# Attention scores of a two-block Macaron network: 32-row matmuls in the exponential pass and a mask matmul in the max pass

## What is computed

```python
def attn(x, wq, wk, wv, wo, bo):            # T = 2048, 16 heads, 8 numbers a head
    q, k, v = split_heads(x @ wq), split_heads(x @ wk), split_heads(x @ wv)
    scores = jnp.einsum('bhqd,bhkd->bhqk', q, k)
    scores = jnp.where(tril(ones((T, T))), scores, -jnp.inf)
    attn = softmax(scores / sqrt(8), axis=-1)
    return merge(jnp.einsum('bhqk,bhkd->bhqd', attn, v)) @ wo + bo
# the second attention is the same, with biased projections and without wo
```

## Time and profile before

| | |
|---|---|
| Time, median of 3 runs | 1313.72 us (1313.71 to 1315.61) |
| Span of the profiled execution | 1311.0 us, first to last instruction |
| Median of the runs above that span | 2.7 us |
| TensorE busy | 1194.1 us, 91% |
| VectorE busy | 1044.4 us, 80% |
| ScalarE busy | 723.5 us, 55% |
| Mean granted TensorE clock | 0.975 of full speed |

### The profile page before, as it was taken

The page is one execution under the profiler, slowest core; times in us unless marked ns, Lnnn a source line. Parts: engine busy times, 40 slices in busy tenths (PEclk is TensorE's granted clock), DMA queues, the critical chain, the costliest instruction groups (busy, mean ns, idle before and its releaser), DMA issues.

```text
span 1311.0 us, 21446 instructions
## 1 busy us (share of the span) xinstructions
PE 1194.1 (91%) x7781; PEld 510.1 (39%) x7781; DVE 1044.4 (80%) x3015; ACT 723.5 (55%) x861; POOL 66.6 (5%) x64
## 2 busy tenths in 40 slices
PE   1999958999999999999699979599999999999997
PEld 1455533333333333334455537233333333333336
DVE  8976588999999887875447567799999989878764
ACT  1322115566777777777332224156667777777773
POOL 5111010000000000000101000100000000000000
PEclk9999979999999999999799989799999999999999
DMA  4100142000000000000000000510000000000001
GB/s 147 34 1 1 39 131 58 2 1 2 2 1 1 2 1 2 1 1 2 1 0 1 1 1 25 154 48 2 2 1 2 2 1 1 2 1 2 2 2 33
DMA packets 23510, 23.26 MB, mean 18 GB/s; under 512 B 3134, under 2 KB 21220, under 8 KB 23404
## 3 DMA queue, kind: packets, MB, share of 16 engines
q1 hardware_dynamic: 22252, 18.73, 4.9%
q0 software_dynamic: 1152, 3.15, 0.9%
HBM read 13.20 MB, written 8.39 MB: 16 GB/s over the span
## 4 chain that ended last, share of the span: by engine, by line
PE 70%; DVE 22%; issue 4%; ACT 2%; DMA 1%; SPq 0%; DVEq 0%; ACTq 0%
PE psum L1184 18%; PE psum L1204 17%; PE psum L1164 14%; PE psum L442 9%; DVE part_max L1314 8%; PE psum L466 2%; PE psum L903 2%; PE psum L1171 2%; DVE junk L1320 2%; DVE xn L167 1%; DVE norm_v L150 1%; PE psum L1224 1%; PE psum L918 1%; DVE norm_stats L141 1%; PE psum L427 1%
## 5 line engine op out<-in xcount | busy, mean ns | idle before, releaser
L1275 ACT ACTIVATE hidden<-psum,exp_scale 128x1024 f32<-128x1024 f32 (+3 forms) x640 | 597.7, 984 | 258.9 <-PE psum L1164 137.3
L1314 DVE TENSOR_REDUCE part_max<-psum 128x1 f32<-128x512 f32 x768 | 492.1, 686 | 59.1 <-PE psum L1204 53.9
L1204 PE MATMUL psum<-k_slots,q_slots 128*128 128x512 f16 (+3 forms) x1280 | 401.2, 356 | 34.2 <-DVE part_max L1314 12.2
L1164 PE MATMUL psum<-q_slots,k_slots 128*128 128x512 f16 (+3 forms) x1280 | 330.9, 348 | 6.3 <-ACT hidden L1275 3.5
L1184 PE MATMUL psum<-hidden,v_aug 128*9 128x512 f32 (+3 forms) x2560 | 293.7, 531 | 0.1
L1320 DVE CUSTOM_DVE_ANT_0 junk<-psum,causal_add 128x384 bf16<-128x384 f32 (+3 forms) x512 | 230.6, 488 | 49.0 <-PE psum L1204 45.9
L1204 PEld LDWEIGHTS psum<-k_slots,q_slots 128*128 128x128 f16 x1280 | 114.5, 97 | 361.1 <-DVE part_max L1314 177.5
L442 PE MATMUL psum<-parts,w_parts 128*128 128x512 f16 x768 | 180.4, 387 | 1.9 <-DVE parts L843 1.9
L1164 PEld LDWEIGHTS psum<-q_slots,k_slots 128*128 128x128 f16 x1280 | 118.3, 98 | 97.8 <-ACT hidden L1275 13.9
L442 PEld LDWEIGHTS psum<-parts,w_parts 128*128 128x128 f16 x768 | 73.7, 99 | 83.1 <-issue 6.8
L586 ACT CAST parts<-psum 128x512 f16<-128x512 f32 x64 | 37.2, 588 | 107.2 <-PE psum L427 107.2
(11 more groups left out here) (170 smaller groups left out, 730.5 us busy)
## 6 DMA issues: line engine op xcount, KB each, us to landing
q_slots<-q_rows SPq DMA_DIRECT2D x8, 512.0 KB, 3.7
k_slots<-k_rows POOLq DMA_DIRECT2D x24, 128.0 KB, 4.1
q_rows<-parts SPq DMA_DIRECT2D x18, 128.0 KB, 2.7
k_rows<-parts SPq DMA_DIRECT2D x18, 128.0 KB, 2.4
q_slots<-in_L_ffn_W_dram SPq DMA_DIRECT2D x2, 1024.0 KB, 6.5
k_slots<-k_rows SPq DMA_DIRECT2D x8, 128.0 KB, 3.9
q_slots<-nm_parts SPq DMA_DIRECT2D x64, 4.0 KB
out_dram<-x_res SPq DMA_DIRECT2D x4, 256.0 KB, 2.3
```

What stands on the lines that cost most here:

```text
L1164: last = pe.matmul(psum[:, S_BANKS + 2 * (tile % 2) + par, off:CH], k_slots[:, G * g + 2 * pr + par, j * P:(j + 1) * P], q_slots[:, g, c * ...
L1204: last = pe.matmul(psum[:, bank, 0:w], q_slots[:, g, qb * P:(qb + 1) * P], k_slots[:, G * g + h, kc * CH:kc * CH + w], start=True, stop=True)
L1275: act.activation(probs[:, tile % NP, :, off:CH], psum[:, bank:bank + 2, off:CH], ACT.Exp, scale=exp_scale[:, layer:layer + 1]).then_inc(ex ...
L1314: dve.tensor_reduce(dst, psum[:, bank, :], axis=AX.X, op=ALU.max).then_inc(ring_read, 1)
```

## The change

The score matmuls of the exponential pass (L1164) read only the 32 partitions of their own head, for weights and for moving data, in place of all 128. The two heads of a tile stand in different 32-row groups of the array and still write two different banks. The mask matmuls behind them stay 128 rows high.

In the max pass, each unit on the diagonal gets a second matmul of 128 columns (`later_keys` against `ident_bf`) that adds the mask in PSUM, and VectorE takes a plain maximum for every unit. The tile `causal_add`, its two GpSimd instructions, the tile `junk` and the wait for it go.

```diff
@@ score_tile @@
                     for par in range(2):
+                        rows = rows_of(2 * pr + par)
                         last = pe.matmul(psum[:, S_BANKS + 2 * (tile % 2) + par, off:CH],
-                                         k_slots[:, G * g + 2 * pr + par, j * P:(j + 1) * P],
-                                         q_slots[:, g, c * CH + off:(c + 1) * CH],
+                                         k_slots[rows, G * g + 2 * pr + par, j * P:(j + 1) * P],
+                                         q_slots[rows, g, c * CH + off:(c + 1) * CH],
                                          start=True, stop=q not in diagonal)
@@ new helper @@
+            def rows_of(h):
+                return slice(SLOT * h, SLOT * (h + 1))
@@ ring_item @@
                         last = pe.matmul(psum[:, bank, 0:w], q_slots[:, g, qb * P:(qb + 1) * P],
-                                         k_slots[:, G * g + h, kc * CH:kc * CH + w], start=True, stop=True)
+                                         k_slots[:, G * g + h, kc * CH:kc * CH + w], start=True, stop=kc < c)
+                        if kc == c:
+                            last = pe.matmul(psum[:, bank, i * P:w], later_keys[:, :], ident_bf[:, :],
+                                             start=False, stop=True)
@@ VectorE @@
-                            if kc < s[1]:
-                                dve.tensor_reduce(dst, psum[:, bank, :], axis=AX.X,
-                                                  op=ALU.max).then_inc(ring_read, 1)
-                            else:
-                                w = (i + 1) * P
-                                if junk_used[n % 2]:
-                                    dve.wait_ge(ring_read, junk_used[n % 2])
-                                dve.tensor_tensor_reduce(out=junk[:, n % 2, 0:w], in0=psum[:, bank, 0:w],
-                                                         in1=causal_add[:, CH - w:CH], scale=1.0,
-                                                         scalar=-3.0e38, op0=ALU.add, op1=ALU.max,
-                                                         accum_out=dst).then_inc(ring_read, 1)
-                                junk_used[n % 2] = n + 1
+                            w = CH if kc < s[1] else (i + 1) * P
+                            dve.tensor_reduce(dst, psum[:, bank, 0:w], axis=AX.X, op=ALU.max).then_inc(ring_read, 1)
@@ GpSimd, start of the kernel (the waits for the masks count one less) @@
-                    pool.memset(causal_add[:, :], 0.0).then_inc(masks_zeroed, 1)
...
-                    pool.affine_select(out=causal_add[:, CH - P:CH], in_=causal_add[:, CH - P:CH],
-                                       compare_op=ALU.is_ge, fill=NEG, base=0, pattern=[[-1, P]],
-                                       channel_multiplier=1).then_inc(masks_done, 1)
```

More of the change, by code:

```diff
@@ L87, in macaron_layers @@
         ident_bf = sb("ident_bf", [P, P], BF16)
-        causal_add = sb("causal_add", [P, CH])
         later_keys = sb("later_keys", [P, P], BF16)
@@ L471, in weights_max @@
                 def weights_max():
-                    pe.wait_ge(masks_done, 6)
+                    pe.wait_ge(masks_done, 5)
                     pe.wait_ge(router_loaded, 32)
@@ L602, in _ @@
                     pool.memset(ident_bf[:, :], 0.0).then_inc(masks_zeroed, 1)
-                    pool.memset(causal_add[:, :], 0.0).then_inc(masks_zeroed, 1)
                     pool.memset(later_keys[:, :], 0.0).then_inc(masks_zeroed, 1)
                     pool.memset(ones_mat[:, :], 1.0).then_inc(masks_done, 1)
-                    pool.wait_ge(masks_zeroed, 4)
+                    pool.wait_ge(masks_zeroed, 3)
                     pool.affine_select(out=ident[:, :], in_=ident[:, :], compare_op=ALU.not_equal, fill=1.0,
@@ L661, in choose @@
                     if first and n == 0:
-                        dve.wait_ge(masks_done, 6)
+                        dve.wait_ge(masks_done, 5)
                     rank_b = rank[:, :].rearrange("p (a e) -> p a e", a=1).broadcast_to([P, BPC, E])
@@ L1072, in attention_layer @@
             recip = sb("recip", [P, 2, BPC, G])
-            junk = sb("junk", [P, 2, CH], BF16)
             part_max = sb("part_max", [P, 2, G, BPC, NCH])
@@ L1080, in attention_layer @@
             k_landed = [sem(f"k_landed{n}") for n in range(1, NCH)]
+            def rows_of(h):
+                return slice(SLOT * h, SLOT * (h + 1))
             def load_k_rows(engine, n, h):
                 cols = slice(n * CH, (n + 1) * CH)
-                return engine.dma_start(k_slots[SLOT * h:SLOT * (h + 1), h::G, cols],
+                return engine.dma_start(k_slots[rows_of(h), h::G, cols],
                                         slot_dram[1].rearrange("(g h) i d t -> h (i d) g t", h=G)[h, :, :, cols])
@@ L1294, in _ @@
                     proj.values_out(dve, n)
-                junk_used = [0, 0]
                 for turn, (items, (m_now, _, _, _)) in enumerate(zip(RING_ITEMS, PLAN)):
```

## The result

The changed kernel takes 1339.09 us (median of 4 runs, 1338.74 to 1342.22) against 1313.95 for the kernel before: ratio 1.0194, 95% interval 1.0182 to 1.0206. It is 25 us slower; the forecast was 15 slower, 1329, with a range of 1307 to 1345. The profiled execution has a span of 1336.9 us, 25.9 more than before.

A forecast was written before the change was run, and what follows sets the result against it. TensorE was taken to bound the middle of the attentions, sharing the limit with VectorE ahead of that. Terms +12.1 - 1 - 2 + 6.5 + 2 - 2 - 0.7 gave +15 us: 1326 profiled, 1329 as median, range 1307 to 1345.

The forecast's parts named there:

- the likeliest case: Overlap works, switches cost 0.09 us as read, the masks are the loss: 1329 us, own range 1317 to 1342, chance 0.68.
- What bounds: Mid-attention TensorE, busy 99.4%, has no slack, so added work reaches the end; ahead of that VectorE shares the limit.
- middle stretches: From 328 to 574 and 984 to 1230 us, mid-attention; masks there were to cost 12.1 us in full.
- Part 1, the saving: In the score tiles, two heads' 32-row matmuls overlap, 0.007 us apart, saving 113 us on TensorE.
- Part 1, the switch: Changing tile height around score tiles costs 0.093 us each way; 1212 switches make 112.7 us on TensorE.
- Touching tiles: 31 pairs of adjacent unmasked score tiles could run four matmuls at once: at most 6.5 us saved, 2 taken.
- Part 2 and 3, masks and VectorE: Max pass: 512 mask matmuls add 28.5 us on TensorE, counted +12.1 and +6.5; plain maxima on VectorE save 2.
- Part 4, the start: Two GpSimd instructions go from before the clearing of `k_slots`, so the first statistics step ends 0.7 us earlier.
- A cheaper switch: Rival: the way from a 128-row matmul into a 32-row tile is free, giving 1284 us; chance 0.13.
- No overlap: Rival: the 32-row score matmuls save nothing and pay 113 us of switches, giving 1434 us; chance 0.07.
- the rest hides it: Rival: adjacent score tiles overlap fully and masks outside mid-attention cost nothing: -1 us, 1313 us; chance 0.12.
- What would show it: Signs in the profile after, among them 0.09 us switches, off-diagonal turns of 2.75 us instead of 2.80.

The follow-up runs named there:

- mask_only: Changed kernel with its score matmuls put back to 128 rows, keeping the mask matmuls and plain maxima: 1329.42 us, ratio 1.0111 to the kernel before.
- mask_twice: Changed kernel with the mask matmul of every diagonal unit made two times: 1359.43 us, ratio 1.0339 to the kernel before.
- rows64: Changed kernel with score matmuls 64 rows high, both heads of a tile reading the same 64 partitions: 1432.01 us, ratio 1.0894 to the kernel before.
- rows_only: Kernel before with only the 32-row score matmuls added, its max pass unchanged: 1327.72 us, ratio 1.0097 to the kernel before.
- before_x: Kernel before, 128-row score matmuls, ring items cut in two places instead of three so score tile 1 stands directly before `values`: 1350.07 us, ratio 1.0271.
- rows_wide_z31: Kernel before with 32-row score matmuls in 512-column tiles only, a quad's score tiles side by side, ring items 3 to 1 around `values`: 1293.84 us.
- rows_wide_z: Kernel before with 32-row score matmuls in 512-column tiles only, a quad's score tiles side by side, ring items halved around `values`: 1283.64 us.

## Why the prediction was right, and where it was off

The direction was right and 1339 lies in the range, but the account behind it held in part only. Forecast were +15 us, measured +25. The term for the 32-row tiles was off by some 12 us. The masks came out near their sum (15.7 against 16.6) by two errors that cancel, which is luck. The own range of the likeliest case reached to +24 on the ground that the masks might cost everywhere; +25 was reached in another way.

*What bounds.* Right in the main. The middle stretches had little slack on TensorE, but not none: there 104 mask matmuls of 0.056 us (5.8 us) added 4.1 us to the first layer's way from the first exponential of step (0, 3) to that of (2, 1), 232.5 us before and 236.6 in mask_only. I had counted them in full, and 70% came through. Over the whole kernel it was 0.040 of 0.056 for the second mask in mask_twice, also 70%.

*Part 1, the saving.* Right. The overlap is full (0.003 us apart), and rows64 shows no other saving: without it 93 us came, of the 113 that were counted on TensorE.

*Part 1, the switch: the term that was mis-sized.* "The price ... is 0.093 us each way, whatever the pair", and the overlap's 0.007, made the 32-row tiles cost -0.5 in all, -1 as they entered the sum (+1 with the touching tiles left out). Measured alone they cost 13 us, 11 of them inside the attentions. A visit takes 0.095 + 0.101 + 0.010 = 0.206 and the overlap 0.003, together 0.016 more than my 0.193. Worked out again: 448 x (-0.007) + 64 x (0.047 + 0.10 + 0.153) = +16, less 68 spared switches of 0.10, +9. The first term had been worth -10. In a balance of 113 us against 113 an error of 0.016 in 0.193, 8%, on one side is 10 us. The middle stretches, where I took -3 with the touching tiles, shrank by 0.4 together; the larger part of the 12 us came in the steps outside them. The 0.010 could be read before: the finer starts had 0.227 behind the first L452, not 0.216, and I passed over it. The 2 us between 9 and 11 the clock accounts for. In the second layer of rows_only it fell to half speed for 3.4 us from 861.6 and again from 940.1, and the steps in which that happened, (0, 0) and (0, 2), took 14.24 and 38.91 us, where the same steps of the first layer took 13.64 and 37.32 at the full clock: 2.2 us. In the kernel before, both layers take the same for these steps (13.3 and 36.7). One `values` there took 1.80 us in place of 1.04:

```profile
939.94 1.80 PE L1188 MATMUL psum<-hidden,v_aug 128*9 128x512 f32 x8
```

At the end of the first layer rows_only had 12.0 us of half speed where the kernel before had 3.4; what that cost I haven't separated, so the 9 may be a little high. The changed kernel's profile, too, has more half speed inside the attentions, 13.6 us against 3.4 before. At half speed TensorE loses at most half of such time, so by this estimate at most 5 us of the 25 came that way.

*Touching tiles.* I took 2 us of at most 6.5. Of the 31 such pairs 17 started all four matmuls together, worth 17 x 0.21 = 3.6; in rows_only it was 12.

*Part 2 and 3, masks and VectorE.* The sum is near, its split is not: 16.6 in the sum (12.1 + 6.5 - 2), 15.7 measured in the attentions of mask_only. In the middle it was 8.3 for 12.1, outside 7.4 for 4.5. Between all and nothing I had taken half for the outside; more than half came. VectorE's own busy time hardly changed, 1044 to 1042 us. (The least distance of the fused instructions is 0.606 us and not 0.610; no term changes by it.)

*Part 4, the start.* Right, 0.7 us.

*The rivals.* A cheaper switch: the way in costs 0.096, so it isn't free. No overlap: shown false, and rows64 gave its time, 1432 against the 1434 worked out. That the rest hides it: partly true for the masks, and not enough. The lower end of the likeliest case, +5, does not follow from its words: the terms of the middle make 12.1 - 1 - 2 = +9, and +5 needs the full overlap of the touching tiles as well.

*What would show it.* Turns off the diagonal were to shorten to 2.75 us; the one shown takes 2.80. The middle stretches were to grow by 4 to 6 us each; the way from step (0, 3) to (2, 1) grew by 4.2 us in the first layer and by 3.8 in the second, and in rows_only by nothing (232.5 in the first, 0.3 less in the second). The switch was to be 0.09: both ways together, with the 0.010 behind them, are 0.206 and not 0.186.

## To carry to other kernels

Short-row matmuls pay by running beside each other, not by being short, and each visit to another tile height has a fixed price (0.206 us here, nearly the 0.216 between the starts of two 512-column matmuls). So count visits first and put as many row groups as there are into each: two heads a visit broke even at 512 columns and lost below; with four heads a visit in the wide tiles alone the kernel was 31 us faster than before. Look too at how the small instructions that feed another engine are spread: the wrong cuts cost more than a switch saved. And moving a mask from VectorE to TensorE is priced by who waits for whom: the add was fused with the maximum and cost VectorE 0.012 us, on TensorE it was an instruction of its own of 0.056.

## What the runs showed of the hardware

- Four 32-row matmuls in four row groups, each into its own bank and each 512 columns long, made one piece of 0.40 us where a single one has 0.38 to 0.39; two were 0.003 us apart.
- The price of a change of tile height did not depend on the number of columns: out of the 32-row tile it was 0.101 or 0.102 us at 512, 384, 256 and 128 columns. Out of the 64-row tile of rows64 it was 0.092 (0.308 less 0.216).
- A matmul that follows directly on the first one after a switch starts 0.010 us late (0.066 in place of 0.056 behind 128 columns, 0.226 in place of 0.216 behind 512).
- How the small ring items are spread over a turn counts: the same instructions, cut in two places instead of three, cost 35 us (before_x), and cut 3 to 1 around `values` instead of 2 to 2 they cost 10 (rows_wide_z31 against rows_wide_z).
- A `values` of eight 9-column matmuls that takes 1.04 us at the full clock took 1.80 where the clock fell to half speed.
